# Attention kernel: the sums products move to ticks 11 and 15, into the ticks of two value batches, and the inversion of the sums three ticks later

## Chip, core and metric

The kernel runs on one core of a Trainium2 chip. The metric is the device time of one execution in microseconds (us). Engines: PE is TensorE (PEld its weight loads), DVE is VectorE, ACT is ScalarE, POOL is GpSimd, SP issues the DMAs.

## What is computed

A block with adaptive layer norm on x of shape 4 x 1024 x 1024: `x = x + ga * attention(h)`, then `x = x + gb * linear(h)` with a LoRA part. The change touches only the attention, for each of 4 batches, 8 key/value heads and 4 query heads on each:

```python
att = einsum('bhgqd,bhkd->bhgqk', q, k) / sqrt(32)
att = where(causal, att, -inf)
probs = softmax(att, axis=-1)
ctx = einsum('bhgqk,bhkd->bhgqd', probs, v)
```

All of it is in float32. The kernel stores the unnormalized context and the row sums of the exponentials, inverts the sums for a whole batch at once, and multiplies them in before the output projection.

## The kernel before

**Three phases** follow each other: the projections (`qkv`, to 0.62 ms), the attention (0.62 to 1.72 ms), and the output projection with the linear half (`linear_half`, to the end). The attention runs over 32 groups (NG), a group being one key/value head of one batch with its four query heads.

**One list orders the attention.** `group_steps(n)` (L105) writes out the steps of group n in NE = 20 ticks, and every engine walks the same list `STEPS` and takes from it what is its own. Each engine works in order; semaphores join them. A tick u holds, in this order:

- `scores` of unit u: PE multiplies the transposed scores of one key block for two or four heads (L1122, two matmuls in most ticks), DVE adds the causal mask on the diagonal units (L1030, units 0 to 5 and 14 to 19), ACT takes the exponentials (L976 or L972). There are SS = 2 score buffers in PSUM; ACT must have read a buffer before PE fills it again.
- `max` of about two units m of the next group (m = 0 to 37; in the last ticks those of the group after that). PE multiplies the scores once more, queries on the partitions (`max_product`, L253, with a mask product on L256 or L251), and DVE reduces them to row maxima (L272, or L269 with the mask in one pass, which ends in a small read of the accumulator). From m = 37 DVE goes on to `max_split` (L278 to L286). In ticks 8 to 11 stand m = 25 to 32, two per tick; in ticks 12 to 14 m = 33 to 37; in ticks 15 to 19 m = 0 to 9 of the group after next.
- `sum`, in tick 9 for the second half of the queries of group n-1 (hf = 1) and in tick 16 for the first half of group n (hf = 0) (`SUM_AT`, L90). PE multiplies a column of ones with the exponentials that POOL has added up (`sums`, L1168; 8 records on L1175 and, for hf = 1, 8 on L1180 of 128 columns). ACT copies the result out (`take_sums`, L989) and SP stores it.
- `turn` in tick 17 (L1166): the row maxima of the next group are transposed, ACT takes them (L996), and SP puts them into the stack that `scores` of the next group reads.
- `inv_in`, `inv`, `inv_out` in ticks 9, 12 and 15 (`INV_AT`, L94), only in groups 8, 16 and 24: SP loads all sums of the finished batch, DVE takes the reciprocal (L1064), SP stores it.
- `values`, in batches of two quads in ticks 1, 5, 7, 11, 15 and 19: PE multiplies exponentials and values into the context (L1143, 16 records). After them POOL adds the exponentials of the quads into `p_sum` (L1082), 15 adds in a group.

`values` and `sums` use 32 columns of the PE array for each of the four heads, in four column tiles that work side by side; `scores`, `max` and `turn` use all 128.

**Small products share three PSUM banks.** `max`, `turn`, `sum` and `mod` take the banks in turn, in the order of the list. A step may start on PE once the step three before it has been read out, by DVE for a `max`, by ACT for a `sum` or `turn` (`wait_bank`, L814):

```python
SMALL = [s for s in STEPS if s[0] in ("max", "turn", "sum", "mod")]
BANK = {s: i % MS for i, s in enumerate(SMALL)}
BEFORE = {s: SMALL[i - MS] if i >= MS else None for i, s in enumerate(SMALL)}
```

So the sum in tick 9 waits for max 26 (it stands behind max 26, 27, 28), and the sum in tick 16 waits for max 1 of the group after next (behind max 1, 2, 3). `sums` waits also for POOL's adds of its half (L1169) and for the last exponentials of that half.

The order within a tick is set by these lines of `group_steps`:

```python
for hf in range(2):
    at = n - 1 if hf else n
    if u == (SUM_AT if n < NG - 1 else SUM_AT_LAST)[hf] and 0 <= at < NG:
        steps.append(("sum", at, hf))
```

Of the kernel before, what the change touches and what calls it, by code (L numbers as in the profile page):

```python
# [86 lines left out]
QS = 3  # L87
SS, MS = 2, 3
LAG = 2
SUM_AT = {1: 9, 0: 16}  # L90
SUM_AT_LAST = {1: 6, 0: 12}
AHEAD = 5
TURN_AT = 17
INV_AT = (9, 12, 15)  # L94
FETCH_AT, FIRST_AT, LORA_AT = (25, 2), (26, 3), (28, 13)
SCALE_AT, SPLIT_HI_AT, SPLIT_LO_AT, COEF_AT = (26, 12), (27, 10), (28, 3), (29, 10)
PARTS = [(2, 4), (3, 9), (4, 14), (5, 19)]
# [7 lines left out]
def group_steps(n):  # L105
# [3 lines left out]
    for u in range(NE):  # L109
# [5 lines left out]
# [4 lines that stand above are left out]
        if n + 1 < NG and u == TURN_AT:  # L119
            steps.append(("turn", n + 1))  # L120
        if n % KV == 0 and 0 < n < NG and u in INV_AT:
            steps.append((("inv_in", "inv", "inv_out")[INV_AT.index(u)], n // KV - 1))
        for kind, at in (("fetch", FETCH_AT), ("first", FIRST_AT), ("scale", SCALE_AT), ("split_hi", SPLIT_HI_AT),
# [1543 lines left out]
```

## Time and profile before

| what | us |
|---|---|
| median of 3 runs | 2493.68 (2493.58 to 2498.49) |
| the profiled execution, its own time | 2495.66 |
| its span, first to last instruction | 2493.9 |
| PE busy in the span | 2406.7 (97%) |
| DVE busy | 1723.4 (69%) |
| POOL busy | 1650.8 (66%) |
| ACT busy | 1042.6 (42%) |

The busy shares are averages over the three phases, which have different limits. A busy PE counts each matmul from its start to its modelled end, and matmuls overlap, so the distance from one start to the next says more than busy time. The attention repeats itself group by group, so one group can be read for all.

### The profile page before, as it was taken

The numbers are of one execution on the slowest core, as the hardware profiler recorded it, in microseconds if no ns is written. First come the engines' busy times: TensorE is split into PE (matmuls) and PEld (weight loads), VectorE is DVE, ScalarE is ACT, GpSimd is POOL, SyncE is SP. The second block draws the span as 40 slices with busy tenths as digits, with TensorE's granted clock in tenths as the row PEclk, the third lists the DMA queues.
The fourth block names the chain that finished last, engine by engine and source line by source line (L and its number), as shares of the span: only waits on it lengthen the run. The fifth ranks groups of instructions, "written<-read, shape, count | busy, mean of one in ns | idle before, by whom it ended". The sixth has DMA issues, their size and how long they took to land. (4 is left out here: it accounts for less than half of the span.)

```text
span 2493.9 us, 36376 instructions
## 1 busy us (share of the span) xinstructions
PE 2406.7 (97%) x13140; PEld 1668.3 (67%) x13204; DVE 1723.4 (69%) x3392; ACT 1042.6 (42%) x1873; POOL 1650.8 (66%) x865
## 2 busy tenths in 40 slices
PE   5999999999999999999999999998999999999998
PEld 3788888887555555555555555544788788888886
DVE  4866666677888888888888888874555355455553
ACT  3433333231666666666666666665211111111111
POOL 3744333441799998999989999993655455545643
PEclk8999999999999999999999999999999999999999
DMA  6532333352545325344233345313333333323330
GB/s 236 198 118 87 115 113 118 123 150 80 162 100 146 82 64 154 83 132 97 71 79 83 83 117 132 84 31 127 112 92 101 103 90 97 118 86 104 107 93 25
DMA packets 179727, 267.45 MB, mean 107 GB/s; under 512 B 20508, under 2 KB 113884, under 8 KB 178400
## 3 DMA queue, kind: packets, MB, share of 16 engines
q1 hardware_dynamic: 179552, 265.13, 36.2%
q8 instruction: 109, 1.79, 0.3%
q14 instruction: 66, 0.54, 0.1%
HBM read 183.22 MB, written 80.81 MB: 106 GB/s over the span
## 5 line engine op out<-in xcount | busy, mean ns | idle before, releaser
L1082 POOL TENSOR_TENSOR p_sum<-p_sum,p_ring 128x1024 f32<-128x1024 f32 (+2 forms) x465 | 991.3, 2164 | 71.0 <-PE ctx_ps L1143 50.2
L976 ACT ACTIVATE p_ring<-scores 128x512 f32<-128x512 f32 (+1 forms) x896 | 448.9, 568 | 236.3 <-DVE scores L1030 173.6
L272 DVE TENSOR_REDUCE neg_max<-scores_q 128x1 f32<-128x512 f32 x679 | 438.8, 684 | 79.0 <-PE scores_q L253 64.9
L253 PE MATMUL scores_q<-k_stack,q_stack 96*128 96x512 f32 (+1 forms) x1473 | 443.0, 378 | 14.6 <-DVE neg_max L269 6.3
L1122 PE MATMUL scores<-q_stack,k_stack 98*128 98x512 f32 (+1 forms) x1216 | 409.7, 414 | 10.6 <-ACT p_ring L976 7.7
L253 PEld LDWEIGHTS scores_q<-k_stack,q_stack 96*128 96x128 f32 x1473 | 263.6, 191 | 135.4 <-DVE neg_max L269 64.5
L1122 PEld LDWEIGHTS scores<-q_stack,k_stack 98*128 98x128 f32 x1216 | 205.9, 190 | 184.7 <-ACT p_ring L976 71.9
L627 POOL TENSOR_TENSOR roped_hilo<-roped_hilo 128x512 fp32r<-128x512 f32 x80 | 105.5, 1319 | 337.0 <-ACT roped_hilo L467 337.0
L269 DVE CUSTOM_DVE_ANT_0 scores_q<-scores_q,masks 128x512 f32<-128x512 f32 x489 | 296.0, 642 | 38.4 <-PE scores_q L253 38.4
L676 PE MATMUL proj_ps<-h_hi,w_hi 128*128 128x512 f32 x752 | 298.7, 397 | 0.7 <-POOL w_lo L616 0.7
L676 PE MATMUL proj_ps<-h_hi,w_lo 128*128 128x512 f32 x752 | 294.1, 391 | 0.0
L676 PE MATMUL proj_ps<-h_lo,w_hi 128*128 128x512 f32 x752 | 293.6, 390 | 0.0
L1514 POOL TENSOR_TENSOR h_scaled<-h_scaled,mod_now 128x512 f32<-128x512 f32 x64 | 65.6, 1046 | 329.9 <-DVE h_scaled L1459 329.8
L1030 DVE TENSOR_TENSOR scores<-scores,consts 128x256 f32<-128x256 f32 (+1 forms) x384 | 201.4, 525 | 61.5 <-PE scores L1122 59.3
L1143 PE MATMUL ctx_ps<-p_ring,v 128*32 128x512 f32 (+3 forms) x2560 | 231.7, 469 | 0.0
L1586 PE MATMUL pf<-we_hi,h_hi 128*128 128x512 f32 x512 | 201.4, 393 | 8.6 <-POOL h_lo L1518 8.6
L1586 PE MATMUL pf<-we_hi,h_lo 128*128 128x512 f32 x512 | 200.9, 392 | 0.0
L1586 PE MATMUL pf<-we_lo,h_hi 128*128 128x512 f32 x512 | 200.9, 392 | 0.0
L1539 PE MATMUL po<-wo_hi,ctx_hi 128*128 128x512 f32 x496 | 196.7, 397 | 1.7 <-issue 1.7
L1539 PE MATMUL po<-wo_hi,ctx_lo 128*128 128x512 f32 x496 | 193.6, 390 | 0.0
L1539 PE MATMUL po<-wo_lo,ctx_hi 128*128 128x512 f32 x496 | 193.5, 390 | 0.0
L455 ACT COPY proj_raw<-proj_ps 128x512 f32<-128x512 f32 x96 | 56.3, 587 | 322.3 <-PE proj_ps L676 321.8
(182 smaller groups left out, 3632.8 us busy)
## 6 DMA issues: line engine op xcount, KB each, us to landing
q_stack<-qk_t SPq DMA_DIRECT2D x96, 512.0 KB, 6.8
qk_t<-roped_hilo SPq DMA_DIRECT2D x80, 512.0 KB, 2.8
x_in<-in_L_attn_resid SPq DMA_DIRECT2D x32, 512.0 KB, 6.3
ctx_t<-ctx_raw SPq DMA_DIRECT2D x64, 256.0 KB, 5.4
prefetched<-in_L_wmod SPq DMA_DIRECT2D x4, 4096.0 KB, 13.6
prefetched<-ctx_t SPq DMA_DIRECT2D x31, 512.0 KB, 4.0
prefetched<-inv_t SPq DMA_DIRECT2D x124, 128.0 KB, 5.5
k_stack<-qk_t SPq DMA_DIRECT2D x96, 128.0 KB, 8.8
```

The lines of the kernel that those rows point to most:

```text
L253: last = nc.tensor.matmul(dst[:, a, :], qs[0:MHI, h, i * P:(i + 1) * P], ks[0:MHI, lo:lo + w], start=not first and (a == 0 or not diag), s ...
L269: nc.vector.tensor_tensor_reduce(row, row, sh.maskW[:, HALF - w:HALF], -1.0, LARGE, ALU.add, ALU.min, neg[:, 0, :]).then_inc(sh.s_mx.sem, 1)
L272: nc.vector.tensor_reduce(neg, src, AX.X, ALU.max, negate=True).then_inc(sh.s_mx.sem, 1)
L627: nc.gpsimd.tensor_tensor(lo, lo.bitcast(F32), qst[r % QST][:, 0, :].bitcast(F32), ALU.subtract).then_inc(s_rl.sem, 1)
L676: last = nc.tensor.matmul(pps[e % PPS][:, :], w[a][c][:, k, :], h[m % 2][i][:, k, :], start=(k == 0 and n == 0), stop=(k == DC - 1 and n = ...
L976: nc.scalar.activation(p[:, a * per:(a + 1) * per, :], src[:, a * per:(a + 1) * per, :], ACT.Exp, scale=SM_SCALE).then_inc(s_ex.sem, 1)
L1030: nc.vector.tensor_tensor(at, at, consts[:, 2 * P:3 * P].rearrange("p (a n) -> p a n", a=1).broadcast_to([P, heads, P]), ALU.add).then_inc ...
L1082: nc.gpsimd.tensor_tensor(a, a, probs(n, u), ALU.add).then_inc(s_ap.sem, 1)
L1122: last = nc.tensor.matmul(o[a], ks[n % QS][0:KS, j * P:(j + 1) * P], qs[n % QS][0:KS, h0:h0 + per, lo:lo + w], start=True, stop=True)
L1143: last = nc.tensor.matmul(cps[DH * h:DH * (h + 1), lo - hf * HALF:HALF], V[:, b % 2, j, g * DH:(g + 1) * DH], p[:, a, :], start=(j == 0), ...
L1539: last = nc.tensor.matmul(po[h][:, :], cs[slot][a][:, k, :], wo[w][:, k, h * HALF:(h + 1) * HALF], start=(k == 0 and n == 0), stop=(k == D ...
L1586: mm = nc.tensor.matmul(pf[h][:, :], hs[a][:, k, :], we[w][:, k, h * HALF:(h + 1) * HALF], start=(k == 0 and n == 0), stop=(k == DC - 1 an ...
```

## The change

It moves the two sums products, with ACT's copy and SP's store of them, to other ticks of the list, and the three steps of the inversion each three ticks later. Nothing is added or removed. The last group (31) keeps its own ticks (`SUM_AT_LAST`), and there `last_sums` does the work. The order of the bank turns follows the list, so the steps that the sums wait for change too: the sum in tick 11 stands behind max 30, 31, 32, the one in tick 15 behind max 37 of the next group and max 0 and 1 of the group after.

```diff
-SUM_AT = {1: 9, 0: 16}
+SUM_AT = {1: 11, 0: 15}
 SUM_AT_LAST = {1: 6, 0: 12}
 AHEAD = 5
 TURN_AT = 17
-INV_AT = (9, 12, 15)
+INV_AT = (12, 15, 18)
```

## Rows read from the trace of the kernel before

**Rows 1.** Busy by stretch, groups 11 and 8: length, PE, PEld, DVE, ACT, POOL, PEclk.

```profile
1002.70:1036.20 33.50, 32.91 (x216) 17.83 (x214) 28.80 (x71) 21.91 (x43) 31.97 (x16) 1.00 0.32 78
...
897.43:932.42 34.99, 32.98 (x216) 17.83 (x214) 30.36 (x72) 21.91 (x43) 33.45 (x16) 1.00 0.33 81
```

**Rows 2.** Timeline of PE, group 11, ticks 9 to 12: start, length, engine, instruction.

```profile
1016.77 0.44 PE L253 MATMUL scores_q<-k_stack,q_stack 96*128 96x384 f32 x1
1017.39 1.07 PE L1175 MATMUL scores_q<-p_sum,ones_v 128*32 128x512 f32 x8 [0.18 <-ACT p_ring L976]
...
1018.61 0.73 PE L1122 MATMUL scores<-q_stack,k_stack 98*128 98x512 f32 x2
...
1020.04 0.69 PE L253 MATMUL scores_q<-k_stack,q_stack 96*128 96x512 f32 x2
1020.66 1.07 PE L1143 MATMUL ctx_ps<-p_sum,v 128*32 128x512 f32 x8
...
1022.51 0.73 PE L1122 MATMUL scores<-q_stack,k_stack 98*128 98x512 f32 x2
1023.09 0.63 PE L253 MATMUL scores_q<-k_stack,q_stack 96*128 96x512 f32 x2
1023.55 0.63 PE L1122 MATMUL scores<-q_stack,k_stack 98*128 98x512 f32 x2
```

**Rows 3.** Timeline of DVE, group 11, ticks 8 to 13.

```profile
1016.02 0.69 DVE L272 TENSOR_REDUCE neg_max<-scores_q 128x1 f32<-128x512 f32 x1 [0.47 <-PE scores_q L253]
...
1017.11 0.14 DVE L269 DVE_READ_ACCUMULATOR2_ANT neg_max<- 128x1 f32 x1
...
1018.14 0.14 DVE L269 DVE_READ_ACCUMULATOR2_ANT neg_max<- 128x1 f32 x1
...
1023.52 0.69 DVE L272 TENSOR_REDUCE neg_max<-scores_q 128x1 f32<-128x512 f32 x1 [1.60 <-PE scores_q L253]
```

**Rows 4.** Timeline of PE, group 11, ticks 15 to 18.

```profile
1026.67 0.28 PE L256 MATMUL scores_q<-masks,ident_b 128*128 128x256 bf16 x1
1026.89 1.92 PE L1143 MATMUL ctx_ps<-p_ring,v 128*32 128x512 f32 x16
1028.74 0.62 PE L1122 MATMUL scores<-q_stack,k_stack 98*128 98x384 f32 x2
...
1029.48 0.42 PE L253 MATMUL scores_q<-k_stack,q_stack 96*128 96x384 f32 x1
1029.84 1.06 PE L1175 MATMUL scores_q<-p_sum,ones_v 128*32 128x512 f32 x8
1030.83 0.62 PE L1122 MATMUL scores<-q_stack,k_stack 98*128 98x384 f32 x2
...
1032.50 1.02 PE L253 MATMUL scores_q<-k_stack,q_stack 96*128 96x384 f32 x2
```

**Rows 5.** Timeline of DVE, group 11, ticks 15 to 18, and tick 0 after it.

```profile
1027.01 0.14 DVE L269 DVE_READ_ACCUMULATOR2_ANT neg_max<- 128x1 f32 x1
...
1028.04 1.28 DVE L272 TENSOR_REDUCE neg_max<-scores_q 128x4 f32<-128x512 f32 x2
1029.39 0.43 DVE L1030 TENSOR_TENSOR scores<-scores,consts 128x256 f32<-128x256 f32 x1
...
1030.85 0.14 DVE L269 DVE_READ_ACCUMULATOR2_ANT neg_max<- 128x1 f32 x1
1031.49 0.43 DVE L1030 TENSOR_TENSOR scores<-scores,consts 128x256 f32<-128x256 f32 x1 [0.50 <-PE scores L1122]
...
1032.30 0.14 DVE L269 DVE_READ_ACCUMULATOR2_ANT neg_max<- 128x1 f32 x1
...
1036.96 0.43 DVE L1030 TENSOR_TENSOR scores<-scores,consts 128x256 f32<-128x256 f32 x1 [0.35 <-PE scores L1122]
```

**Rows 6.** Timeline of POOL, group 11, and of DVE, group 8, tick 12.

```profile
1021.90 22.33 POOL L1082 TENSOR_TENSOR p_sum<-p_sum,p_ring 128x1024 f32<-128x1024 f32 x10 [1.03 <-PE ctx_ps L1143]
...
919.47 1.75 DVE L1064 RECIPROCAL prefetched<-prefetched 128x256 f32<-128x256 f32 x1
```

## The prediction

> **What bounds the kernel now.** I read the busy time by stretch first. Group 11 takes 33.50 us, with PE busy for 32.91, POOL for 31.97, DVE for 28.80 and ACT for 21.91, at full clock [rows 1]. Nothing is far from the bound, so busy shares can't settle a move of about one microsecond per group. The timelines of PE and DVE can. In them group 11 and group 12 have the same length, and 22 of the 32 groups last 33.5 us; most others hold `mod` or `inv` or lie at the ends. What one group shows counts some 30 times.
>
> In the timelines PE and DVE pace each other. From 1023.52 to about 1029.3 DVE has no idle time over 0.1 us; it then has two waits for PE's scores, 0.50 us before 1031.49 and 0.35 us before 1036.96 [rows 4, 5]. Between them it runs without a pause, and PE waits for it: the product of max 6 starts at 1032.50, 0.06 us after the read at 1032.30 has ended that frees its bank [rows 4, 5]. From there the products up to the values batch of tick 19 follow DVE, and the next group's scores follow that batch. So there is one loop of both engines, and a delay of DVE at 1031.49 delays the whole next group. POOL has 1.03 us per group to spare: it waits for the first values of tick 11 [rows 6].
>
> **What a sum costs PE by itself.** The values batch of tick 15 has 16 records and lasts 1.85 us to the next scores (1026.89 to 1028.74), the 8 records of the sum in tick 16 0.99 us (1029.84 to 1030.83) [rows 4]. The difference of 8 records is 0.86 us, so 0.13 us of either is no record's. The first two scores after a tiled block take 0.58 us (1022.51 to 1023.09), two products in a plain place 0.46 (1023.09 to 1023.55): 0.12 us more. The last two before a block take 0.62 (1020.04 to 1020.66): 0.16 more [rows 2]. Together 0.41 us for a block that stands alone, and a sum that leads directly into a values batch should not pay it. That is 61 moved sums (31 of hf 0, 30 of hf 1), 25 us at most. The Trainium skill says the same in kind: "TensorEngine Tiling (Array Packing)", Key Properties, has PE drain when the tiling mode changes, and by that rule alone the kernel would be about 25 us faster. The rows bear out that there is such a cost. They also show waits that the rule leaves out.
>
> **Sum of hf 1, tick 9 to 11.** Now it is held by DVE. The last product before it starts at 1016.77, just after the end of the reduction that frees its bank (1016.02 + 0.69), the sum at 1017.39; the sum's bank came free with the accumulator read at 1017.11, ended 1017.25. So PE starts a sum 0.14 us after DVE frees its bank [rows 2, 3]. After the change ticks 8 to 11 have eight products in a row, and no block between them lets DVE catch up. Two reductions of 384 columns take 1.03 us (1017.11 to 1018.14), one of 512 columns lasts 0.69 [rows 3]. DVE would take max 29 at 1018.14, max 30 at 1018.65, and end it at 1019.34. PE would start scores 10 at 1016.95 (a product of 384 columns takes three quarters of the 0.23 of 512, 0.18), product 30 at 1017.82 instead of 1017.60 (it waits for max 27, which is read out by 1017.77), scores 11 at 1018.05, product 32 at 1018.85. The sum waits for max 30: 1019.34 + 0.14 = 1019.48, where without the bank it would start at about 1019.24. The sum takes 1.22 - 0.13 = 1.09 us (1017.39 to 1018.61) and the values 1.85 (1020.66 to 1022.51) [rows 2]. Scores 12 then start at 1022.42 in place of 1022.51. **Gain 0.1 us**, in place of 0.41, since two DVE holds take the rest. Bounds: 0 (another 0.1 us of hold) and 0.41.
>
> **Sum of hf 0, tick 16 to 15.** Now it stands behind max 3 and waits for max 1, long done. Placed before the values of tick 15 it waits for max 37. DVE ends that at 1027.15 (1027.01 + 0.14) [rows 5]. I give all of this part in the times of before and take the 0.10 off at the end. PE has finished issuing at 1026.67 and would start a tiled block at 1026.89, as now [rows 4]; the sum starts at 1027.15 + 0.14 = 1027.29, **a new stall of 0.40 us**. Then 0.86 us of sum and 1.85 of values: scores 16 start at 1030.00, in place of 1028.74, 1.26 later.
>
> Of this DVE gives back a part. It has only max 0 and 1 left for this long block, ends them at 1029.32, and idles until scores 16 come: mask 16 starts 0.65 us after scores 16 (1028.74, 1029.39), so at 1030.65, an idle time of 1.3 us that was under 0.1 [rows 4, 5]. From mask 16 on, DVE needs 1.46 us for mask 16, max 2 and max 3 (1029.39 to 1030.85, where the last read begins and the next instruction could), then it can take mask 17 at 1032.11. It does so at 1031.49 now, after waiting 0.50 us for PE, whose sum in tick 16 lies in between. That wait goes: PE starts scores 17 0.92 us after scores 16 (0.74 to max 3's product, 1028.74 to 1029.48, and 0.18 for it), at 1030.92, and they are ready by 1031.5, before DVE is. So DVE's chain from mask 17 on stands at +0.62 us against now, and with the 0.10 off at **+0.52 us**. PE's saved entry and exit of the sum in tick 16 are hidden behind DVE there. `turn` and max 5 wait for banks of max 3 and max 2 that DVE frees late; the product of max 6 starts at 1033.02 in place of 1032.50, and all up to scores 0 of the next group moves with it [rows 4, 5].
>
> Bounds of this part, hf 0 alone: with no stall for max 37 it would be +0.22 (0.62 - 0.40), with 0.15 us more of latencies +0.77. I take +0.62, as every term stands in rows of this stretch.
>
> **The rest of the lists.** ACT copies the sum of tick 15 behind the exponentials of that tick; what scores 17 need of ACT, the exponential of unit 15, stands before the copy, and the next exponential waits for scores 16 anyway. ACT idles about a third of the group [rows 1]. SP stores the sums 2 ticks later and 1 tick earlier, past the context stores and the stack rows of the turn, none of which waits for it. The exponential of unit 15 needs the sum of hf 1 for its ring place, four ticks later; POOL's four adds of hf 0 end at 1020.87 (1021.90 - 1.03) in group 11 and the last one of hf 1 stands before them, so at about 2.2 us each (22.33 / 10) it ends near 1013 [rows 6]; neither sum waits for POOL. I cost all of these at nothing; if POOL fell behind by its 1.03 us, each would still have some 5 us. `inv` moves too: in group 8 the reciprocal of 1.75 us stands in tick 12, where DVE has no pause until tick 16, and the group lasts 34.99, 1.49 more [rows 1, 6]. In tick 15 it stands right before the new idle time of 1.3 us; it takes about 1.67 us of DVE, so about 0.3 is left (with the 0.1 that it starts earlier): **gain 1.2 us, three times**. SP's load of the sums follows the store in tick 11 by one tick, now three, and DVE's demand for it is some 6 us later.
>
> **Sum.** Groups 1 to 29 +0.52, group 0 +0.62, group 30, which has no products of a group after next and so less DVE work, about -0.5: 15.1 + 0.6 - 0.5 = 15.2. Less 3 x 1.2 = 3.6: +11.6 us. Against the profiled span of 2493.9 us this is 2505.5 (its execution's own time was 2495.66, so 2507.3); the median of the runs lies 0.2 below the span, and I forecast **2505.3 us**.
>
> **Rivals.**
> 1. PE sets the pace alone, and the drains count: 61 x 0.41 = 25 us and the 3.6 of the inversion, 2465. For it: PE is busy for 32.91 of 33.50 us. Against it: the holds at 1017.39 and 1032.50. A half of it (hf 1 gains 0.41, hf 0 costs nothing) gives 2478. Chance 0.13 for anything over 5 us faster.
> 2. The sum in tick 15 hardly waits for max 37, or DVE finds idle time I don't see: +0.22 - 0.10 = +0.12 per group, 3.5 us, less 3.6 of the inversion: 2493.6, no change. Against it: the sum in tick 9 does wait for its bank by the same rule. Chance 0.15.
> 3. Slower still: the turn of tick 17 comes 0.5 us later, and ACT and SP bring its rows to the stack late for scores 0. Now there is no idle time of PE ahead of scores 0 at 1036.20. It decides if the turn slips by more against scores 0 than its margin, which I put at half a microsecond or more; then 0.3 us more per group, 2515. Chance 0.07.
>
> My forecast has 0.65. Its own range is +0.52 with 0.12 to either side in 30 groups, 2501.5 to 2509. For 8 in 10 the range has to take in rival 2: **2491 to 2511**. About 0.2% (5 us) is what a measurement of this kernel can tell from no change: faster 0.14, within it 0.16, slower 0.70.
>
> **What would show it.** A group like 11 lasts 34.0 us. On PE's row of L1175 an idle time or a late start in tick 15, about 0.6 us after the last mask product instead of 0.22; values following without a gap. On DVE an idle time of 1.3 us before mask 16, none before mask 17. Groups 8, 16 and 24 last about 0.3 us more than their neighbours, not 1.5. POOL's wait before tick 11's adds grows from 1.03 to 1.5. I would be wrong if DVE keeps a wait before mask 17 (then PE sets the pace there), if the sum in tick 15 starts 0.22 us after the last product, or if a values block behind a sum pays the 0.13 us again.

## The result and the profile after

The changed kernel takes 2510.2 us (median of 6 runs, 2504.38 to 2511.88), the kernel before 2493.63 (6 runs, 2492.46 to 2499.21): ratio 1.0053, 95% interval 1.0037 to 1.0068. It is slower by half a per cent. The forecast was 2505.3, with 2501.5 to 2509 as its own range and 2491 to 2511 as the wide one: the median lies just outside the first and inside the second.

Where the time went is told by three stretches of each profile, the phases cut at the first scores of group 0 and of group 31. Columns: bounds, length, then PE, PEld, DVE, ACT and POOL busy, granted clock, DMA share, GB/s. The kernel before:

```profile
0.00:621.39 621.39, 592.03 (x2770) 481.19 (x2774) 422.15 (x668) 201.98 (x317) 240.74 (x160) 0.99 0.39 134
621.39:1680.98 1059.59, 1031.94 (x6748) 559.90 (x6809) 898.96 (x2172) 681.58 (x1337) 986.40 (x464) 1.00 0.38 100
1680.98:2493.90 812.92, 782.71 (x3622) 627.22 (x3622) 402.28 (x553) 159.07 (x220) 423.68 (x242) 0.99 0.32 96
```

And the changed kernel:

```profile
0.00:623.28 623.28, 594.45 (x2774) 482.25 (x2774) 422.13 (x668) 201.92 (x317) 240.53 (x160) 0.98 0.39 134
623.28:1695.57 1072.29, 1033.72 (x6809) 568.31 (x6810) 891.92 (x2172) 677.35 (x1337) 987.14 (x465) 1.00 0.38 99
1695.57:2509.70 814.13, 783.96 (x3622) 627.15 (x3622) 399.60 (x553) 158.97 (x220) 422.32 (x241) 0.99 0.33 96
```

Groups 0 to 30 take 12.7 us more (1059.59 to 1072.29), which is the change. The projections before them, whose code and order are the same, take 1.9 more at a mean clock of 0.98 in place of 0.99; the rest from group 31 on takes 1.2 more. These 3.1 us can't be laid to the change: in the ten profiles of kernels with full work, the experiments below included, the projections last from 620.8 to 625.5 us and the rest from 806.7 to 814.7. That is also why the sections below go by the length of a group first and by whole times second. The fastest runs of both kernels differ by 11.9 us.

Groups 11 and 8 after, the same view as [rows 1]:

```profile
1009.42:1043.49 34.07, 32.93 (x218) 18.10 (x214) 28.56 (x71) 21.77 (x43) 31.95 (x16) 1.00 0.31 78
903.84:938.06 34.22, 32.93 (x218) 18.09 (x214) 30.06 (x72) 21.77 (x43) 32.11 (x16) 1.00 0.33 80
```

A plain group takes 34.07 us in place of 33.50, a group with an inversion 34.22 in place of 34.99. Now PE's timeline of group 11 in ticks 11 and 15 to 18, which answers to [rows 2, 4]:

```profile
1025.36 0.73 PE L253 MATMUL scores_q<-k_stack,q_stack 96*128 96x512 f32 x2
1026.22 1.06 PE L1175 MATMUL scores_q<-p_sum,ones_v 128*32 128x512 f32 x8
...
1027.30 1.07 PE L1143 MATMUL ctx_ps<-p_sum,v 128*32 128x512 f32 x8
...
1029.15 0.73 PE L1122 MATMUL scores<-q_stack,k_stack 98*128 98x512 f32 x2
...
1033.32 0.28 PE L256 MATMUL scores_q<-masks,ident_b 128*128 128x256 bf16 x1
1033.94 1.06 PE L1175 MATMUL scores_q<-p_sum,ones_v 128*32 128x512 f32 x8 [0.33 <-DVE neg_max L269]
1034.79 1.93 PE L1143 MATMUL ctx_ps<-p_ring,v 128*32 128x512 f32 x16
1036.65 0.62 PE L1122 MATMUL scores<-q_stack,k_stack 98*128 98x384 f32 x2
...
1039.04 0.30 PE L1166 MATMUL scores_q<-consts,neg_max_hilo 128*128 128x128 f32 x1 [0.18 <-DVE neg_max L269]
...
1039.79 1.01 PE L253 MATMUL scores_q<-k_stack,q_stack 96*128 96x384 f32 x2
```

In tick 15 the sum starts 0.62 us after the last product (1033.32 to 1033.94), where a tiled block started 0.22 after it [rows 4]; the profile names DVE's L269 as what it waited for. The sum itself takes 0.85 us to the values, and the values 1.86 to the next scores: the 0.85 us hold no entry or exit, so the two blocks pay for one entry and one exit together. DVE in the same stretch, which answers to [rows 5]:

```profile
1033.65 0.14 DVE L269 DVE_READ_ACCUMULATOR2_ANT neg_max<- 128x1 f32 x1
...
1034.68 1.28 DVE L272 TENSOR_REDUCE neg_max<-scores_q 128x4 f32<-128x512 f32 x2
1037.31 0.43 DVE L1030 TENSOR_TENSOR scores<-scores,consts 128x256 f32<-128x256 f32 x1 [1.35 <-PE scores L1122]
...
1038.75 0.14 DVE L269 DVE_READ_ACCUMULATOR2_ANT neg_max<- 128x1 f32 x1
1038.75 0.47 DVE L1030 TENSOR_TENSOR scores<-scores,consts 128x256 f32<-128x256 f32 x1
```

The read of max 37 ends at 1033.79 and the sum starts 0.15 us later. DVE then stands idle for 1.35 us before mask 16, and mask 17 follows max 3 without a pause (1038.75), where it had waited for PE.

### The profile page after: what moved, and what is told of

It reads as the page before. It is cut to its first block and busy times, and to the rows that moved or that the text cites. A ratio compares the mean times of both kernels' runs of the same rounds, so it can differ in the third digit from the quotient of the medians.

```text
span 2509.7 us, 36440 instructions
## 1 busy us (share of the span) xinstructions
PE 2412.1 (96%) x13204; PEld 1677.7 (67%) x13204; DVE 1713.7 (68%) x3392; ACT 1038.2 (41%) x1873; POOL 1650.0 (66%) x865
## 5 line engine op out<-in xcount | busy, mean ns | idle before, releaser
L253 PE MATMUL scores_q<-k_stack,q_stack 96*128 96x512 f32 (+1 forms) x1473 | 459.7, 383 | 12.5 <-DVE neg_max L269 2.2
L1122 PE MATMUL scores<-q_stack,k_stack 98*128 98x512 f32 (+1 forms) x1216 | 404.0, 409 | 10.1 <-ACT p_ring L976 7.1
L269 DVE CUSTOM_DVE_ANT_0 scores_q<-scores_q,masks 128x512 f32<-128x512 f32 x489 | 294.2, 643 | 0.0
```

Source lines behind the costliest of these rows:

```text
L253: last = nc.tensor.matmul(dst[:, a, :], qs[0:MHI, h, i * P:(i + 1) * P], ks[0:MHI, lo:lo + w], start=not first and (a == 0 or not diag), s ...
L269: nc.vector.tensor_tensor_reduce(row, row, sh.maskW[:, HALF - w:HALF], -1.0, LARGE, ALU.add, ALU.min, neg[:, 0, :]).then_inc(sh.s_mx.sem, 1)
L1122: last = nc.tensor.matmul(o[a], ks[n % QS][0:KS, j * P:(j + 1) * P], qs[n % QS][0:KS, h0:h0 + per, lo:lo + w], start=True, stop=True)
```

## Experiments

Each was run beside the kernel before on one chip, and a ratio compares the two there. The kernel before took 2497.15 us (24 runs) beside the first four experiments, 2498.08 (11 runs) beside the light kernels and the versions that beat both, and 2496.45 (one run) beside the other two. The length of a group or tick is the distance from its first scores to the next one's on PE's timeline; where no group is named it is group 11.

### One sum at a time

```diff
-SUM_AT = {1: 11, 0: 15}
+SUM_AT = {1: 9, 0: 15}
```

> The sum of hf 0 alone is moved (16 to 15) and the sum of hf 1 stays in tick 9; the inversion as in the changed kernel. Theory (the sum in tick 15 waits 0.4 us for max 37, and DVE stands idle behind the long block, so that mask 17 comes 0.66 us later; the move of hf 1 gains 0.10): a plain group lasts 33.50 + 0.66 = 34.16 us, 0.10 longer than with both moved; about 2512 us for a kernel whose other phases last as in the changed kernel's profile. Rival A (the loss comes from the sum of hf 1, which reaches ACT, the ring and POOL two ticks later): a plain group lasts 33.1 to 33.5 us, and the kernel 2485 to 2494.

Measured: 2508.54 us (5 runs, 2506.22 to 2515.44), ratio 1.0047 (1.0028 to 1.0066).

```diff
-SUM_AT = {1: 11, 0: 15}
+SUM_AT = {1: 11, 0: 16}
```

> The sum of hf 1 alone is moved (9 to 11), hf 0 stays in tick 16; the inversion three ticks later. Theory: a plain group lasts 33.40 us, 0.10 less than before, since the hold for max 30's bank takes most of the 0.41 us of entry and exit; 2490 us. If no bank held the sum, the group would be 33.1 and the kernel 2481. Rival A (the loss comes from hf 1): 34.0 us and about 2509.

Measured: 2492.91 us (10 runs, 2490.70 to 2497.76), ratio 0.9988 (0.9978 to 0.9998). Group 11 by stretch, hf 0 alone and then hf 1 alone, and below that group 8 of the latter:

```profile
1014.21:1048.35 34.14, 32.99 (x218) 18.07 (x214) 28.65 (x71) 21.80 (x43) 31.95 (x16) 1.00 0.31 77
```

```profile
1003.21:1036.63 33.42, 32.81 (x218) 17.86 (x214) 28.67 (x71) 21.89 (x43) 32.02 (x16) 1.00 0.31 75
898.93:933.14 34.21, 33.12 (x217) 17.88 (x213) 30.06 (x72) 21.77 (x43) 32.77 (x16) 1.00 0.32 79
```

With hf 0 alone a group is 0.64 us longer than before, with hf 1 alone 0.08 shorter; together they make the 0.57 of the change. Expected were 34.16 and 33.40, measured 34.14 and 33.42. Rival A, that the loss comes with hf 1, is out: the whole loss comes with the move of hf 0. It begins in tick 15, which lasts 4.70 us with hf 0 alone in place of 3.44; ticks 16 to 19 give back 0.62 of these 1.26.

### The inversion alone

```diff
-INV_AT = (9, 12, 15)
+INV_AT = (12, 15, 18)
```

> The inversion alone three ticks later, both sums where they were. Theory: the reciprocal now stands before mask 16, where DVE has an idle time under 0.1 us in this order of steps and 0.5 us before mask 17, so of its 1.67 us about 1.0 is left on the path: groups 8, 16 and 24 last 34.5 us instead of 34.99, the others 33.50; the total within 2 us of before. In the changed kernel these groups last 34.22, 0.15 over their neighbours, because DVE is idle for 1.35 us there. Rival (the reciprocal costs less in tick 15 whatever stands beside it): 33.7 us here too.

```profile
896.85:931.19 34.34, 33.23 (x217) 17.86 (x214) 30.16 (x72) 21.79 (x43) 32.78 (x16) 1.00 0.33 78
```

Measured: 2495.31 us in one run, beside 2497.15 for the kernel before, which says nothing of 2 us; the group says more. Group 8 takes 34.34, a plain group 33.51. So 0.83 us of the reciprocal is left on the path in place of 1.49 (expected 1.0, and 0.2 by the rival, which is out). In the changed kernel 0.15 is left (34.22 against 34.07), as there DVE is idle for 1.35 us in that place. The cost of the reciprocal goes by DVE's idle time beside it, if not to the tenth: 0.8 us of it is hidden here, where DVE's two idle times make 0.6 [rows 5].

### The sums behind the values

The block on PE keeps its place and its length, only the order within it is turned round, so the wait for the bank falls while the values run. In `group_steps` the loop that appends the sums stands behind the one that appends the values:

```diff
-        for hf in range(2):
-            at = n - 1 if hf else n
-            if u == (SUM_AT if n < NG - 1 else SUM_AT_LAST)[hf] and 0 <= at < NG:
-                steps.append(("sum", at, hf))
...
         if 0 <= at < NG and v == QUADS[QUAD_OF[v]][-1] and QUAD_OF[v] % BATCH == BATCH - 1:
             steps += [("values", at, q) for q in range(QUAD_OF[v] - BATCH + 1, QUAD_OF[v] + 1)]
+        for hf in range(2):
+            at = n - 1 if hf else n
+            if u == (SUM_AT if n < NG - 1 else SUM_AT_LAST)[hf] and 0 <= at < NG:
+                steps.append(("sum", at, hf))
```

> As the changed kernel, sums in the same ticks 11 and 15, but each behind the values batch of its tick in place of ahead of it. The tiled block on PE keeps its length and its place; only the wait for the bank falls behind 1.85 us of values. Theory (waits of 0.19 us for max 30 and 0.40 us for max 37 hold PE): no idle time of PE before either block, a plain group of 34.06 - 0.19 - 0.40 = 33.47 us, 2490 us. Rival B (the length of the block in tick 15 starves DVE, whatever holds PE, and costs all of it): 34.0 us and 2508. Between the two, the difference to 34.06 is the share of the hold.

Measured: 2494.07 us (12 runs, 2488.56 to 2502.33), ratio 0.9990 (0.9977 to 1.0003). PE's timeline of group 11 of that kernel, tick 15, and below it that group by stretch:

```profile
1028.21 0.28 PE L256 MATMUL scores_q<-masks,ident_b 128*128 128x256 bf16 x1
1028.42 1.92 PE L1143 MATMUL ctx_ps<-p_ring,v 128*32 128x512 f32 x16
1030.16 1.04 PE L1175 MATMUL scores_q<-p_sum,ones_v 128*32 128x512 f32 x8
1031.14 0.62 PE L1122 MATMUL scores<-q_stack,k_stack 98*128 98x384 f32 x2
```

```profile
1004.54:1037.98 33.44, 32.79 (x217) 17.88 (x213) 28.55 (x71) 21.88 (x43) 31.95 (x16) 1.00 0.33 79
```

The values start 0.21 us after the last product, the whole block ends 0.40 us sooner after it (2.93 against 3.33), and a group takes 33.44 us; 33.47 was expected. The wait for max 37's bank is a wait, and worth what its length says: tick 15 lasts 4.30 us in place of 4.71, and ticks 16 to 19 last 6.84 to 6.85 in both orders. In tick 11, where hf 1 waited for max 30, the turned order takes 4.06 in place of 4.26. Rival B is out as the whole of it. The turned order also hands POOL the values sooner, but POOL waits for them in both kernels (1.61 us before tick 11's adds, and 0.98 with the order turned), and 0.61 of the 0.63 us gained stands in the two ticks with a hold. The same for hf 0 alone (`SUM_AT = {1: 9, 0: 15}` in this kernel):

> The sum of hf 0 in tick 15 behind the values, the sum of hf 1 in tick 9 as before. Theory: of the 0.66 us that the move of hf 0 costs a group, the wait for max 37's bank is 0.39; 0.26 is DVE's idle time behind the longer block, less the entry and exit that PE saves. A plain group lasts 33.76 us. Rival (hold and idle time overlap, so that without the hold nothing is lost): 33.5 us. If the falls of TensorE's clock come with a sum behind the values of tick 15, they show here too, in tick 19 (1.6 us each).

```profile
1006.25:1040.06 33.81, 32.96 (x218) 17.93 (x214) 28.67 (x71) 21.89 (x43) 31.97 (x16) 1.00 0.33 77
```

The plain groups of this run last between 33.73 and 33.81 us (group 7 apart, in which the clock fell), as expected: 33.76. The median plain group takes 33.50 us before, 34.14 with hf 0 ahead of the values and 33.77 with hf 0 behind them. So of the 0.64 us that the move of hf 0 costs, 0.37 is the hold. The other 0.27 goes with the place, in either order; the forecast had put it at 0.22. With hf 0 behind the values nothing holds the block, and DVE still stands idle before mask 16 in group 11:

```profile
1033.87 0.43 DVE L1030 TENSOR_TENSOR scores<-scores,consts 128x256 f32<-128x256 f32 x1 [0.95 <-PE scores L1122]
```

DVE is idle here for 0.95 us. In the kernel before it is idle for under 0.1 us at this place and for 0.50 us before mask 17 [rows 5]; that second wait is gone here, as in the changed kernel. That the 0.27 us is what this idle time leaves after PE's saving is read from these rows; no run has the one without the other. The whole run took 2502.53 us.

### DVE and POOL made light

The kernels before and after, each with less work for DVE and POOL and the same order of steps. They leave out most of each row maximum and of each sum and so compute something else; the exponent is scaled otherwise so that nothing overflows. Two places of the edit:

```diff
-    src = bank[:, 0:len(hs) * w].rearrange("p (h n) -> p h n", h=len(hs))
+    src = bank[:, 0:len(hs) * w].rearrange("p (h n) -> p h n", h=len(hs))[:, :, 0:64]
...
-                nc.gpsimd.tensor_tensor(a, a, probs(n, u), ALU.add).then_inc(s_ap.sem, 1)
...
+                nc.gpsimd.tensor_tensor(a, a, probs(n, u)[:, :, 0:64], ALU.add).then_inc(s_ap.sem, 1)
```

> The kernel before, with DVE and POOL made light: DVE reduces only the first 64 columns of each product of the maxima, POOL adds only the first 64 columns of each block of exponentials, and the exponent's scale is 0.001 so that nothing overflows. The order of all steps is that of before. Theory: no product waits for DVE, so a plain group falls from 33.50 to about 32 us and is PE's own length.

> The changed kernel, with DVE and POOL made light in the same way. Theory (the changed order loses only by DVE's holds and DVE's idle time): with DVE light, the sums keep what they save on PE, and a plain group is shorter than that of the light kernel before by up to 2 x 0.41 = 0.8 us (by 0.4 at least, as ACT needs 0.98 us per tick in full ticks). Rival C (a sum ahead of a values batch costs something on PE or ACT itself): equal or longer than the light kernel before.

Measured: 2439.36 and 2421.01 us, one run each. Group 11 of the light kernel before, then of the light kernel after:

```profile
987.07:1018.73 31.66, 31.43 (x214) 17.99 (x214) 14.36 (x70) 21.64 (x43) 7.51 (x15) 1.00 0.35 82
```

```profile
980.07:1011.14 31.07, 30.88 (x214) 18.18 (x214) 14.36 (x70) 21.54 (x43) 7.53 (x15) 1.00 0.35 83
```

The sign turns. With DVE and POOL out of the way the changed order is the faster one, by 0.59 us per group and 18 us in all; with their full work it is the slower one by 0.57. So the saving on PE's entries and exits is there to be had (the forecast's rival 1 had the right mechanism; it put it at 2 x 0.41 = 0.82 per group, of which 0.59 shows), and DVE and POOL together take it away twice over. Rival C, that a sum ahead of a values batch costs something on PE or ACT itself, is out. Which of the two is told by the waits above and not by this pair: PE's rows name DVE, and POOL still waits for PE (1.61 us before tick 11's adds in the changed kernel, 1.03 before [rows 6]).

### A version that beats both

The sum of hf 1 in tick 11 behind the values (the loop of the sums stands behind that of the values, as above), hf 0 back in tick 16, and the reciprocal in tick 11 of the group after, where DVE is idle anyway:

```diff
-SUM_AT = {1: 11, 0: 15}
+SUM_AT = {1: 11, 0: 16}
...
-        if n % KV == 0 and 0 < n < NG and u in INV_AT:
-            steps.append((("inv_in", "inv", "inv_out")[INV_AT.index(u)], n // KV - 1))
+        for kind, off, tick in (("inv_in", 0, 12), ("inv", 1, 11), ("inv_out", 1, 15)):
+            if n % KV == off and KV <= n < NG and u == tick:
+                steps.append((kind, n // KV - 1))
```

> The sum of hf 1 in tick 11 behind the values, the sum of hf 0 in tick 16 as before, and the reciprocal in tick 11 of the group after (DVE was idle there for 2.9 us in the changed kernel). Theory: hf 1 gains 0.10 + 0.19 = 0.29 us per group, a plain group lasts 33.2 us, and groups 8, 16 and 24 no more than that, nor 9, 17 and 25: 2493.6 - 30 x 0.29 - 3 x 1.5 = 2480 us, if TensorE's clock is not halved for a while as it was six times in the kernel with both sums behind the values (1.6 us each).

```profile
997.71:1030.94 33.23, 32.78 (x218) 17.77 (x214) 28.67 (x71) 21.89 (x43) 31.97 (x16) 1.00 0.33 77
894.81:928.04 33.23, 32.78 (x218) 17.77 (x214) 28.67 (x71) 21.88 (x43) 31.99 (x16) 1.00 0.33 81
```

Measured: 2483.57 us (6 runs, 2479.21 to 2487.78), ratio 0.9944 (0.9927 to 0.9960). The groups last 33.2 as expected, with no trace of the inversion in groups 8, 16 and 24, nor in the groups after them. The whole was expected at 2480 from the 2493.6 of the first comparison; the kernel before took 2498.08 beside it. (The expectation counts six falls of the clock in the kernel with both sums behind the values; its profile has five in groups 1 to 30, and one in group 0, which every profile has.) This version is faster than the kernel before by over half a per cent, and than the changed one by over one, if the two ratios may be set against each other (0.9944 and 1.0053).

One step further, on PE alone, the sum of hf 0 and scores 17 change places:

```diff
-            for step in STEPS:
+            order = list(STEPS)
+            for n in range(NG - 1):
+                k = order.index(("sum", n, 0))
...
+                order[k], order[k + 1] = order[k + 1], order[k]
+            for step in order:
```

> As the run before, and on PE alone the sum of hf 0 comes behind scores 17 in place of ahead of it (every other engine keeps its order, banks and waits are the same). Theory (DVE waits 0.5 us for scores 17 behind the sum, and all that follows waits for DVE): mask 17 starts up to 0.6 us earlier, the products of max 4 and 5 come behind the sum and then hold DVE, so about 0.2 us per group is left as a gain: 33.0 us, 2475. Rival (PE alone sets the pace in ticks 16 to 19): no difference to the run before.

Measured: 2481.95 us (6 runs, 2480.28 to 2483.91), ratio 0.9939 (0.9924 to 0.9954), groups of 33.23 as in the run before: no difference that can be told, which was the rival's forecast. The expectation of a gain failed. (Group 30 is the exception, with 32.14 us in place of 31.23.) Of this kernel, PE's row of the turn in group 11:

```profile
1028.02 0.30 PE L1167 MATMUL scores_q<-consts,neg_max_hilo 128*128 128x128 f32 x1 [0.25 <-ACT prob_sums L990]
```

and ACT's copy of the sum:

```profile
1027.29 0.58 ACT L990 COPY prob_sums<-scores_q 128x512 f32<-128x512 f32 x1 [0.57 <-PE scores_q L1176]
```

and DVE's mask 17, max 4 and mask 18:

```profile
1026.82 0.47 DVE L1031 TENSOR_TENSOR scores<-scores,consts 128x256 f32<-128x256 f32 x1
1027.63 0.57 DVE L270 CUSTOM_DVE_ANT_0 scores_q<-scores_q,masks 128x384 f32<-128x384 f32 x1 [0.35 <-PE scores_q L254]
...
1028.83 0.70 DVE L1031 TENSOR_TENSOR scores<-scores,consts 128x512 f32<-128x512 f32 x1
```

DVE's wait before mask 17 did go, and max 4 started 0.17 us earlier, counted from scores 16 at 1024.71 (2.92 us after them; 3.09 in the kernel before [rows 4, 5], where mask 17 stands at 1031.49 plus 0.34 for it, from 1028.74, and 3.09 in the run before as well). But the turn shares the sum's bank. ACT ends its copy 3.16 us after scores 16, in the run before 2.82, and the turn starts 3.31 us after them in place of 2.96. Scores 18 stand behind it, and mask 18 starts where it did (4.12 after scores 16, 4.08 in the run before). I had left out the turn's own wait.

## Why the prediction was right

**The step that decided.** "... the sum starts at 1027.15 + 0.14 = 1027.29, a new stall of 0.40 us": the start came 0.62 us after the last product in place of 0.22, a stall of 0.40, with DVE named as its cause. Turning the order round took 0.39 to 0.41 out of tick 15 and nothing out of the ticks behind it.

**DVE's idle time.** Forecast 1.3 us before mask 16 and none before mask 17; the rows show 1.35 and none. From scores 16 to mask 17 it was to be 2.11 us and is 2.10 (1036.65 to 1038.75). The move of hf 0 was to cost +0.62 and costs 0.65 in group 11: scores 16 come 1.27 us later in place of 1.26, and of that ticks 16 to 19 give back 0.62 in place of 0.64. A small miss of size, in the ticks behind mask 17.

**The sum of hf 1.** Forecast gain 0.10 us. Ticks 8 to 11 take 7.39 us in place of 7.49, and hf 1 alone shortens the median plain group by 0.09. The hold for max 30 is the one that was reckoned: DVE begins max 30, of 0.69 us, at 1025.39, and the sum starts at 1026.22, 0.14 us after its end.

**The inversion.** Forecast 0.3 us left of 1.49; 0.15 is left. Group 8 of the changed kernel on DVE:

```profile
929.09 1.28 DVE L272 TENSOR_REDUCE neg_max<-scores_q 128x4 f32<-128x512 f32 x2
930.28 1.74 DVE L1064 RECIPROCAL prefetched<-prefetched 128x256 f32<-128x256 f32 x1
931.94 0.41 DVE L1030 TENSOR_TENSOR scores<-scores,consts 128x256 f32<-128x256 f32 x1
```

DVE's next instruction starts 1.66 us after the reciprocal, as reckoned. The idle time it fills is 1.35 us and not the 1.3 I took, and it starts 0.09 before the reductions end: mask 16 comes 2.85 us after these reductions began, where it comes 2.63 after them in group 11 (1034.68 to 1037.31). So 0.22 is left at mask 16. Where the last 0.07 us goes behind it I leave open.

**Group 30.** This term was wrong. "Group 30 ... about -0.5": it lasts 31.50 us in place of 31.48. PE's tick 16 does get shorter there (0.46 us in place of 1.54) and tick 15 is not held (3.28 in place of 2.40, which is the sum alone), but tick 17 takes 1.21 in place of 0.48. With few products left, PE runs into the exponentials of ACT, and ACT's copy of the sum now stands ahead of those of tick 16 and not behind them. That this is the cause is argued from the order of ACT's instructions and was not tried. What ends the group is not DVE's work on products either. In both kernels the first scores of group 31 wait for the turn's rows to come by DMA, 1.10 us before and 1.13 after, and they start 3.1 us after ACT has begun to read the turn (at 1677.92 before and at 1692.48 after). The row after:

```profile
1695.57 1.21 PE L1122 MATMUL scores<-q_stack,k_stack 98*128 98x512 f32 x4 [1.13 <-DMA q_stack<-neg_max_rows]
```

**The sum.** Groups 0 to 30 were to take 11.6 us more and take 12.7: 0.04 more in each of 29 groups, 0.5 more in group 30, about 0.4 less in the inversions. That these misses partly cancel is luck. Between that and the 16.6 us of the medians lie 3.1 us of the profiled pair outside these groups and 0.8 us more that no profile shows; the clock has a part in the projections (from 20 to 90 us its mean is 0.85 after and 0.88 before). The changed and unchanged kernels' fastest runs are 11.9 apart. So the size was right for the mechanism and 5 us short for the median.

**The rivals.** Rival 1 (PE alone): its saving exists, as the light pair shows, and is covered. By the rule of the Trainium skill ("TensorEngine Tiling (Array Packing)", Key Properties) a change of tiling mode drains PE; the traces agree, with 0.41 us for an entry and an exit and none between a sum and the values behind it. Rival 2 (hardly a wait for max 37) is refuted by the row, rival 3 (the turn too late for scores 0) did not come: tick 19 lasts 2.85 us in both. POOL's wait before tick 11's adds grew to 1.61 us, where 1.5 was expected.

## What to carry to other kernels

When two engines pace each other through a few banks, the worth of moving a step is read from the slack of both at the old and at the new place, and above all from which earlier step holds the bank that it takes there. Put the step that needs a late bank behind the work that it is batched with, not ahead of it. A batch saves switching on the engine that runs it, and starves the other one if it lasts longer than the work that the banks hold for it.

## What was not expected of the hardware

In three of the kernels with a sum of hf 0 in tick 15, TensorE's granted clock falls from 2.4 to 1.2 GHz for 3.4 us in a few groups, always in tick 19. One microsecond of such a fall, in group 3 of the first profile of the kernel with both sums behind the values, by stretch (0.50 is the clock):

```profile
760.00:761.00 1.00, 1.00 (x8) 0.20 (x4) 1.00 (x4) 0.60 (x1) 1.00 (x1) 0.50 0.52 156
```

The same kernel's group 12 by stretch and the values batch of its tick 19, and then the same batch in group 11, at full clock:

```profile
1037.98:1073.06 35.08, 34.45 (x218) 18.05 (x214) 28.96 (x72) 21.89 (x43) 33.60 (x17) 0.95 0.35 83
```

```profile
1069.96 3.16 PE L1143 MATMUL ctx_ps<-p_ring,v 128*32 128x512 f32 x16
```

```profile
1036.34 1.71 PE L1143 MATMUL ctx_ps<-p_ring,v 128*32 128x512 f32 x16
```

> The kernel with both sums behind the values once more, to see whether TensorE's clock is halved in the same groups (3, 12, 14, 16, 20) again. If the falls belong to the program, they come in the same tick 19 of about the same number of groups; if they belong to the single execution, there are other groups or none, and plain groups last 33.46 us in any case.

The group takes 1.6 us more than its neighbours, and most of it stands in the values batch of tick 19, with 3.16 us in place of 1.71. The fall came in groups 3, 12, 14, 16 and 20 in the first profile and 4, 12, 14, 16 and 20 in the second (2498.26 us, where group 12 takes 35.07), so it goes with the program for the most part and hardly with the single execution. With hf 0 alone behind the values it came in groups 7 and 24, with hf 0 alone ahead of them in group 8, and in the profiles of the kernels before and after, of the light kernels and of the two fastest versions in none of groups 1 to 30. So a sum in tick 15 is not enough to bring it: the changed kernel has one. Just before the fall PE has been through ticks 17 and 18 with its short holds for DVE (in group 3 it was busy for 3.54 of the 4 us from 755 to 759 us, and the fall began at 758.9). Why it comes in these groups stays open. Five times 1.6 us make 8 us. Groups 0 to 30 of that kernel take 1063.2 us in both profiles, 3.6 more than in the kernel before, and without the falls they would take some 4 less. How many of its 12 runs had the falls is not on record; the median was 2494.07 where 2490 was expected, and the fastest run took 2488.56.
